# A GNN, linear-attention and mixture-of-experts layer on one core: the mixer's attention rows and queries made one group ahead of its feed-forward, loops written out

## The reference, cut to what matters

```python
xn = _layernorm(x, axis=-1)
x = x + gnn(xn, edge_attr_3, src, dst, ...) + mix(xn[None], ...)[0]
x = x + ffn(_layernorm(x, axis=-1)[None], ...)[0]

# gnn: one message per edge, summed at its destination
m = jnp.concatenate([h[edge_src], w], axis=1)
h_N = jax.ops.segment_sum(jax.nn.relu(m @ W1.T + b1), edge_dst, ...)

# mix: 4 layers over all nodes
for i in range(DEPTH):
    h = _layernorm(x, ln1_g[i], ln1_b[i])
    x = x + _linear_attn(h, Wq[i], Wk[i], Wv[i], Wo[i], bo[i])
    h = _layernorm(x, ln2_g[i], ln2_b[i])
    x = x + (gelu(h @ W1[i] + b1[i], approximate=False) @ W2[i] + b2[i])

# _linear_attn, per head of 32
q = softmax(split(x @ Wq) * scale, axis=-1)
k = softmax(split(x @ Wk) * scale, axis=-2)
context = einsum('bhnd,bhne->bhde', k, v)      # needs every node
out = einsum('bhnd,bhde->bhne', q, context)
```

## Time and profile before

| | |
|---|---|
| median of 3 runs | 2426.01 us (2425.75 to 2429.09) |
| the profiled execution, its own time | 2427.93 us |
| its span (first to last instruction) | 2426.2 us |
| PE, DVE, ACT, POOL busy share | 84%, 64%, 39%, 56% |
| mean granted TensorE clock | 0.921 |
| mixer layers | from about 130 us to 1897 us |

### The profile page before, as it was taken

The page is one execution under the profiler, slowest core; times in us unless marked ns, Lnnn a source line. Parts: engine busy times, 40 slices in busy tenths (PEclk is TensorE's granted clock), DMA queues, the critical chain, the costliest instruction groups (busy, mean ns, idle before and its releaser), DMA issues. The chain is left out here.

```text
span 2426.2 us, 36176 instructions
## 1 busy us (share of the span) xinstructions
PE 2035.1 (84%) x10736; PEld 1661.2 (68%) x10736; DVE 1542.0 (64%) x3503; ACT 951.4 (39%) x1978; POOL 1365.6 (56%) x1118
## 2 busy tenths in 40 slices
PE   2359899998989999898999998899999775699990
PEld 2248677777767777776777777777777564688880
DVE  4658777666876767687777667866766456511116
ACT  1234444443544444443444444444444242133330
POOL 4156666667556666665666666566666400366650
PEclk7769999999999999999999999999999786799995
DMA  8652222224222223332322224222222432599997
GB/s 200 187 136 67 73 67 67 67 67 122 64 71 67 69 72 72 96 83 73 72 67 68 68 71 111 68 66 68 67 71 67 88 96 85 181 302 305 306 289 165
DMA packets 269614, 266.96 MB, mean 110 GB/s; under 512 B 146079, under 2 KB 203510, under 8 KB 269526
## 3 DMA queue, kind: packets, MB, share of 16 engines
q0 software_dynamic: 127488, 134.76, 23.2%
q1 hardware_dynamic: 137926, 131.35, 18.6%
q10 hardware_dynamic: 4112, 0.03, 0.1%
HBM read 229.85 MB, written 35.06 MB: 109 GB/s over the span
## 5 line engine op out<-in xcount | busy, mean ns | idle before, releaser
L780 POOL DMA_INDIRECT G<-P_d,src_T x896 | 1159.2, 1294 | 708.4 <-DVE z L419 428.7
L387 ACT ACTIVATE zr<-z 125x512 fp32r<-125x512 f32 x448 | 275.0, 631 | 551.3 <-DVE z L419 507.9
L419 DVE TENSOR_TENSOR z<-bank,G 125x512 f32<-125x512 f32 x448 | 293.4, 686 | 226.9 <-PE bank L379 96.4
L1190 PE MATMUL bank<-TT,W_s 128*128 128x250 f32 (+1 forms) x1280 | 369.3, 439 | 1.0 <-ACT TT L838 0.9
L1057 PE MATMUL bank<-W_s,hid 128*125 128x256 f32 x1600 | 359.6, 379 | 0.0
L1057 PEld LDWEIGHTS bank<-W_s,hid 128*125 128x125 f32 x1600 | 292.8, 187 | 42.8
L1190 PEld LDWEIGHTS bank<-TT,W_s 128*128 128x128 f32 x1280 | 242.7, 196 | 104.3 <-issue 12.1
L393 DVE SCALAR_TENSOR_TENSOR zl<-z,zr 125x512 fp32r<-125x512 f32 x448 | 288.4, 684 | 8.1 <-ACT zr L387 8.1
L371 PE MATMUL bank<-zr,onehot 125*125 125x256 f32 x896 | 271.3, 334 | 12.8 <-DVE zl L393 12.8
L372 PE MATMUL bank<-zl,onehot 125*125 125x256 f32 x896 | 230.3, 288 | 0.0
L922 ACT ACTIVATE hid<-bank,b1c 128x375 f32<-128x375 f32 x320 | 163.0, 521 | 100.1 <-PE bank L1190 90.5
(11 more groups left out here) (310 smaller groups left out, 3103.4 us busy)
## 6 DMA issues: line engine op xcount, KB each, us to landing
W_s<-in_L_ffn_w SPq DMA_DIRECT2D x64, 512.0 KB
hid<-in_L_ffn_w SPq DMA_DIRECT2D x64, 512.0 KB
G<-P_d,src_T POOLq DMA_INDIRECT x896
W_s<-in_L_mix_W SPq DMA_DIRECT2D x8, 1024.0 KB
aT<-attr_d SPq DMA_DIRECT2D x224, 31.2 KB
attr_d<-hn SPq DMA_DIRECT2D x12, 246.1 KB, 3.7
X<-in_x SPq DMA_DIRECT2D x5, 560.0 KB
P_d<-es SPq DMA_DIRECT2D x25, 112.0 KB
```

What stands on the lines that cost most here:

```text
L387: nc.scalar.activation(zr[:, s, k, :], z[:, k, :], ACT.Relu).then_inc(r_done, 1)
L419: nc.vector.tensor_tensor(z[:, k, :], edge_bank[k][0:ET, :], G[:, ST * s + 2 * k:ST * s + 2 * k + 2, :].rearrange("p j d -> p (j d)"), ALU ...
L780: pool.indirect_dma_start(G[:, j, :], None, P_d[:, :], bass.IndirectOffsetOnAxis(ap=src_T[:, at:at + 1], axis=0)).then_inc(g_in[j], 16)
L1190: ins = pe.matmul(to[:, 0:(b - a) * T], W1_s[:, k, part], TT[:, k, TT_PIECES[pc]], start=k == 0, stop=k == KD - 1)
```

## The change

`second` is dissolved. In the feed-forward section PE's order for group g becomes: blocks f of g with s0 after f=0, s1 after f=2, s2 after f=3, s3 after f=5, s4 after f=7 (`FF_STEP`); first-norm transposes of g+2; query transposes and attention rows of g+1; queries of g+2; output rows piece 0, s5, piece 1, s6, second-norm transposes of g+1 (in the last group: first-norm transposes of the next layer), piece 2, s7. ACT and DVE follow. On DVE the residual and statistics of piece 2, their aggregate and its copy now stand ahead of s7. The middle gets group 0's attention rows and second norm, queries of groups 0 and 1, and 4 steps; the two steps that opened a layer stay in the first layer alone. Each layer's first norm uses statistics that are finished in parts (`deviations`, `inverse_std`). PE's and SP's loops over layers and groups are written out; ACT reads gains and biases where they lie (`lnp`, `b1_s`) in place of copies. Two of the four steps after the layers move into the first layer. No matmul, gather or element of work is added; one ACT copy pair and a full-width `std` a layer go, small `std`s and reciprocals come.

```diff
+        FF_STEP = {0: 0, 2: 1, 3: 2, 5: 3, 7: 4}
...
# PE
-            with pe.Fori(0, L) as l:
+            for l in range(L):
...
+                queries(0)
+                step(eM)
+                pe.wait_ge(cn_done, l + 2)
...
+                normalised_T(l * SETS + set_q1(1) + 0, ring_q1(l, 1))
+                pe.wait_ge(ring_act, uM + 2)
...
+                step(eM + 1)
+                queries_T(0)
+                pe.wait_ge(row_dve, row_ao(l, 0) + 1)
+                attention(0)
+                queries(1)
+                step(eM + 2)
+                normalised_T(l * SETS + set_h2(0), ring_h2(l, 0))
+                step(eM + 3)
...
-                        if f % 2 == 0:
-                            step(f // 2 + 1)
-                    if not last:
-                        normalised(h0 + GT, u0 + GT + LNU + 2 * NF, GT + LNU + 2 * NF)
-                        queries(u0 + GT + LNU + 2 * NF, r0 + NRP, NRP)
-                    step(5)
...
+                        if f in FF_STEP:
+                            step(e0 + FF_STEP[f])
+                    if g + 2 < NG:
+                        normalised_T(l * SETS + set_q1(g + 2), ring_q1(l, g + 2))
+                    if g + 1 < NG:
+                        queries_T(g + 1)
+                        attention(g + 1)
+                    if g + 2 < NG:
+                        queries(g + 2)
...
+                    out_rows(0)
+                    step(e0 + 5)
+                    out_rows(1)
+                    step(e0 + 6)
+                    if g + 1 < NG:
+                        normalised_T(l * SETS + set_h2(g + 1), ring_h2(l, g + 1))
+                    elif l + 1 < L:
+                        normalised_T((l + 1) * SETS, ring_h1(l + 1, 0))
+                    out_rows(2)
+                    step(e0 + 7)
...
# ACT
+                        if f in FF_STEP:
+                            step(e0 + FF_STEP[f])
+                    if g + 2 < NG:
+                        first_norm(ring_q1(l, g + 2), ring_q1(l, g + 2) - RING_A)
+                    if g + 1 < NG:
+                        queries_T(g + 1)
+                        second_std(g + 1)
...
+                    if g + 2 < NG:
+                        q_softmax(g + 2)
+                    step(e0 + 5)
+                    step(e0 + 6)
+                    if g + 1 < NG:
+                        second_norm(g + 1)
...
+                    step(e0 + 7)
# DVE
+                    step(e0)
+                    if g + 2 < NG:
+                        dve.wait_ge(ring_full, ring_h2(l, g) + LNU)
+                        normalised(g + 2)
+                    for i in range(1, 5):
+                        step(e0 + i)
+                    if g + 1 < NG:
+                        attention(g + 1)
+                    if g + 2 < NG:
+                        queries(g + 2)
...
+                    residual(g, r2, 0)
+                    step(e0 + 5)
+                    residual(g, r2, 1)
+                    row_stats(g, r2, 0, st5, a_stat)
+                    step(e0 + 6)
+                    if g + 2 < NG:
+                        q_softmax(g + 2)
+                    residual(g, r2, 2)
+                    row_stats(g, r2, 1, st5, a_stat)
+                    row_stats(g, r2, 2, st5, a_stat)
+                    aggregate(a_stat, a_aggr, l * NT + g * GT + NT, st5, mv5)
+                    keep_stats(g, l * NT + g * GT + NT, a_aggr, a_mv)
+                    step(e0 + 7)
```

More of the change, by code:

```diff
@@ L866, in _, with step @@
                 both(e)
+            def step(ge):
+                act_edges(ge, ge % PG)
             for l in range(L):
[L869 to L875, removed]
@@ new lines, in second_std, with queries_T @@
+                def second_std(g):
+                    act.wait_ge(b_aggr, l * NT + g * GT + GT)
+                    std(std5b[:, :], mv5b[:, :, 1], b_std)
+                def queries_T(g):
+                    u = ring_qT(l, g)
+                    for j in range(GT):
+                        copy_tile(u + j, u + j - RING_A, QT[:, :, j * T:(j + 1) * T], T)
+                if l == 0:
+                    deviations(0, NG, NG)
+                    first_norm(ring_h1(0, 0), 0)
+                    for i in range(ST_A):
+                        step(EG_FIRST * PG + i)
@@ L895, in _ @@
+                    step(step_k(l, g))
                     for j in range(GT):
[L896 to L902 removed]
@@ L903, in _ @@
[L903 to L917 removed]
+                        u = u0 + LNU + 4 + j
@@ L924, in second @@
-                        if f % 2 == 0:
-                            step(f // 2 + 1)
-                    if not last:
-                        normalised(u0 + GT + LNU + 2 * NF, GT + LNU + 2 * NF)
-                    step(5)
-                    if not last:
-                        q_softmax(r0 + NRP, l * NG + g + 1)
-                    step(6)
-                    step(7)
-                for g in range(NG - 1):
-                    second(g)
-                second(NG - 1, last=True)
+                            u = u0 + 2 * f + pc
@@ new lines, in ring, with row_of, rows_at @@
+            def ring(u):
+                pe.wait_ge(ring_act, u - 1)
+                return RING[(u - RING_A) % 3]
+            def row_of(u):
+                pe.wait_ge(row_dve, u)
+                return ROW[(u - ROW_A) % 2]
+            def rows_at(u, i, products):
+                a, b = RP[i]
+                to = row_of(u + i)
+                for j in range(a, b):
+                    pairs = products(j)
+                    for n, (w, m) in enumerate(pairs):
+                        ins = pe.matmul(to[0:T, (j - a) * D:(j - a) * D + D], w, m, start=n == 0, stop=n == len(pairs) - 1)
+                ins.then_inc(row_full, 1)
@@ L1437, in _ @@
                 dve.memset(ctxS[:, :, :], 0.0).then_inc(l_init, 1)
                 dve.memset(mO[:, :], LOW).then_inc(l_init, 1)
[L1439 to L1442 removed]
+                if l == 0:
+                    normalised(0)
+                    for i in range(ST_A):
+                        step(EG_FIRST * PG + i)
                 dve.wait_ge(l_init, l * 2 + 2)
[L1445 to L1447 removed]
+                for g in range(NG):
+                    u0, r0, q0, eg = ring_k(l, g), row_k(l, g), l * (2 * NG) + g * 2, step_k(l, g)
@@ L1575, in _ @@
-                for g in range(NG - 1):
-                    second(g)
-                second(NG - 1, last=True)
+                    r = rM + NRP + h
+                    dve.wait_ge(row_full, r + 1)
+                    dve.tensor_scalar(M_s[:, h, :], ROW[(r - ROW_A) % 2][:, 0:D], rk[:, h:h + 1], None, ALU.mult).then_inc(row_dve, 1)
+                step(eM + 1)
+                attention(0)
+                queries(1)
+                second_norm(0, ring_q1(l, 1) + LNU)
+                step(eM + 2)
```

461 lines of the change are left out of this document (234 added, 227 removed).

## The result

| | before | after |
|---|---|---|
| median | 2427.55 us (2425.75 to 2430.58, 4 runs) | 2554.02 us (2547.77 to 2555.51, 4 runs) |
| ratio | | 1.0506, 95% interval 1.0492 to 1.052 |
| span of the profiled execution | 2426.2 us | 2550.8 us |
| PE, DVE, ACT, POOL busy share | 84%, 64%, 39%, 56% | 81%, 60%, 37%, 54% |

The change costs 126.5 us. I had said 2504 (2432 to 2550): the sign and the cause are right, the size is 50 us short.

The account below looks back on a forecast made before the run. PE, 84% busy, was taken as the bound, with POOL's gathers a near second limit. Middle and feed-forward +110.6, layer changes -29.7, tail -10.8, clock +8 gave 2506 on the profiled 2427.9, so a median of 2504 us (2432 to 2550).

Parts of the forecast that it names:

- the mechanism: Feed-forward groups: POOL's gathers, 6.48 us a step, run unbroken from s7's `z`; PE waits for features behind s4's late data.
- T: Zero point of the forecast's times in a feed-forward group: the end of PE's last output piece.
- Rival (b): Whole kernel: PE keeps its pace, every group drops 3.7 us, 132 us gained in all, 2294 us; chance 0.11.
- the right comparison: Feed-forward group: POOL's run from s7's `z` to s4's data, 29.7 us, against PE's own work there, 22.8.
- step: 38.2: Middle section, from the K section's end to group 0's start point: summed to 38.2 us, ending with a step.
- tail: Steps behind the last layer: two left instead of four, paced by gathers, 20.2 us instead of 31.0, so -10.8.
- loops: PE's loops written out: 0 us, since the old trace showed no idle time between passes.
- So a group takes 70.0: Feed-forward groups 0 to 2, with queries: 70.0 us instead of 64.7; 3.7 of waits go, 9.7 of new ones come.
- +8 (between 0 and 26): PE's low granted clock after new waits: 8 us taken, at most 20 x 1.3 = 26.
- the seam and the K section: Layer change: last rows to first keys 3.6 us instead of 13.5, three times, -29.7, with 3.0 of new waiting.
- +78: Whole kernel: the sum of all terms, +110.6 - 29.7 - 10.8 + 8, on the profiled execution's 2427.9 us.
- rival (d): Whole kernel much slower: clock stays low after longer waits, +26, or SP's `aT` is late, +15; up to 2545; chance 0.07.

Follow-up runs that it names:

- the seam experiment: Steps spread and relus moved, plus on DVE group 1's norm behind the next layer's first two key maxima and V copies, against the kernel without that move: 2395.0 us.

## Why the prediction was wrong in size

**Right: the mechanism.** POOL's run is the path. The prediction's points, with T = 829.92 + 0.11 = 830.03: the run starts at 4.06 (said 3.3) and has no break; s4's last gather is at 27.9 (27.3); its data is read 4.69 later (4.7); the features start at 33.9, where 33.4 was said; the zl wait is 1.18 (1.4), the ROW bank 0.91 (1.0). `z` waits 7.3 us for gathers in the group (over 5). Halving the gathers and spreading the steps each remove the whole gap. Rival (b), PE keeping the pace, was refused on the right comparison. But its price of 132 us is not found where its condition is met: with half the gathers the changed kernel is no faster than the kernel before with half, since waits of 0.62, 1.18, 1.46 and 0.91 us a group stay. Only the spread kernels beat the kernel before, by 1.1 to 1.6%, not by 5%.

**Right by luck: the middle, "step: 38.2".** It takes 38.4 us to the start of its fourth step, PE's timeline in the second layer:

```profile
738.38 0.71 PE L1198 MATMUL bank<-ident,qe 125*128 125x125 f32 x4 [1.97 <-ACT QT L884]
738.92 1.84 PE L1172 MATMUL bank<-M_s,QT 128*125 128x256 f32 x4
...
757.48 1.06 PE L425 MATMUL bank<-Wst,aT 128*125 128x512 bf16 x2
```

The prediction's 38.2 has that step in it, and its group 0 begins with the same step as its s7. So about 1.4 us are counted twice in each layer, and like against like 36.7 stands against 38.4. The miss is of the kind of the others: the attention row takes 1.84 us here and 1.03 at full clock, and the step at 733.05 takes 2.56 where 1.38 was reckoned.

**Right: tail, loops.** Behind the last layer 21.1 us pass (2032.31 to 2053.43) where 20.2 was said and 31.1 stood in the earlier trace rows. Written-out loops gain nothing. The 5.2 us wait for the first norm between layers is gone.

**Mis-sized: the feed-forward groups, "So a group takes 70.0".** They took 71.7 and 71.6 (group 0: 72.5), group 3 64.9 (62.5), group 4 57.3 (54.3): 11.2 us a layer. In the groups with queries the miss has two parts, both in the rows shown. First, `z` of s7 starts at 3.07, not 2.35: the sum left out what DVE issues between the copy and `z`, the register load of the changed order; the row has 0.64 of idle time <-issue there. Secondly, after a wait of 3.22 us the granted clock is low: from 864.6 to 869.0 the windows give it as 0.61, and query transposes with the first attention row take 3.77 us (865.23 to 869.00) where they took 2.36 before (from the first of the earlier trace rows to the row here, where the second attention row begins, PE's timeline of the kernel before; `M_s` is an attention row):

```profile
774.58 1.03 PE L1057 MATMUL bank<-M_s,QT 128*125 128x256 f32 x4
```

PE's timeline of the changed kernel shows the same in group 3, where four matmuls of an attention row take 1.61 us instead of 1.03, and in group 4, where 1.9 us of wait were foreseen and 16 matmuls of output rows take 5.31 us instead of 3.62:

```profile
1007.79 0.71 PE L1198 MATMUL bank<-ident,qe 125*128 125x125 f32 x4 [3.27 <-ACT QT L884]
1008.34 1.61 PE L1172 MATMUL bank<-M_s,QT 128*125 128x256 f32 x4
...
1086.40 0.43 PE L1182 MATMUL bank<-ident,hn 125*128 125x125 f32 x2 [3.07 <-ACT TT L879]
1086.66 5.31 PE L1172 MATMUL bank<-W_s,hid 128*125 128x256 f32 x16
...
1091.92 3.62 PE L1172 MATMUL bank<-W_s,hid 128*125 128x256 f32 x16
```

**Mis-sized: the clock, "+8 (between 0 and 26)".** I had taken it that several waits are on ACT's or POOL's pace, "where a slow PE costs nothing". This is the step that failed most. The long wait *ends* at the features, and what follows it (query transposes, attention rows, queries) is PE's own path. It costs 1.4 us in the rows above, and in each of the 12 groups with queries the same stretch takes 3.55 to 4.03 us, where it took 2.36. An estimate for a layer from rows of the second: three groups with queries at 1.4, group 3 at 1.6, group 4 at 1.7, the K section at 1.5, the middle at 2.9, about 12. That is some 44 us in all (group 4 and the K section have it in three layers), above the bound of 26. The pages bear this out: PE is busy 18.5 us longer for the same matmuls (2053.6 against 2035.1), on top of the 1.3 us a group that the kernel before lost. The digit 9 of the earlier trace rows, which I read as full clock, can't show losses of this size: the mean granted clock of the mixer's layers is 0.96 in both kernels.

**Mis-sized: the seam and the K section.** From the last rows to the end of the K section 94.8 us pass (624.31 to 719.1), where 99.6 - 9.9 = 89.7 was said. PE's timeline at the start of the K section:

```profile
624.31 0.59 PE L425 MATMUL bank<-Wst,aT 128*125 128x512 bf16 x2
...
635.45 1.11 PE L1221 MATMUL bank<-TT,Wk_s 128*128 128x250 f32 x4 [3.65 <-ACT eT L950]
636.40 3.41 PE L1172 MATMUL bank<-Wv_s,TT 128*125 128x256 f32 x8
...
652.00 2.85 PE L1172 MATMUL bank<-Wv_s,TT 128*125 128x256 f32 x12 [0.97 <-DVE ctxS L1641]
...
656.73 1.11 PE L1221 MATMUL bank<-TT,Wk_s 128*128 128x250 f32 x4 [1.03 <-ACT eT L950]
657.67 1.89 PE L1172 MATMUL bank<-Wv_s,TT 128*125 128x256 f32 x8
```

The wait was foreseen in part (3.0 of the 3.65). The low clock behind it was not (eight matmuls of `V` rows in 3.41 us instead of 1.89), nor the second key group's two waits of about 1 us, which the kernel before doesn't have. Those are some 4 of the 5.1 us. The transfer of `aT` was said to be over at T + 12.5; the seam experiment shows it at T + 17.5 (1030.10 against 1012.54 + 0.11). In the changed kernel PE asked at 641.32, T + 17.0, and had no wait in its row: it was hidden only because PE was late too.

**The account.** Short by layer: 8.1, 16.6, 15.2 and 14.5 us, 54.4 in all (layer by layer from the last rows, before and after). Less the +8 that stood for the clock, and with 0.8 by which the tail gave less, that is 47.2 of the 48.5 between +78 and the +126.5 of the medians. The step counted twice made the sum some 5 us larger, so without it the miss would have been about 54. The range's upper end of 2550 stood on rival (d), which had the largest missing piece, a low clock after long waits, at a chance of 0.07. That was not a rival: it follows from the forecast's own waits. Its other piece, a late `aT`, didn't come.

## What to carry to other kernels

Where a slow producer with a shallow buffer feeds steps that are strewn into other work, the spacing of the steps matters as much as their number. With 6.5 us of gathers a step and room for two steps, groups 1 and 2 take 64.1 and 64.0 us when the eight steps are spread, and 71.7 and 71.6 when s7 to s4, six of them, stand within 25 us of PE's own work, with DVE's order the same in both. When a program order is rewritten, write down for each engine what stands directly behind the instruction that may be late: here the same late `z` cost some 40 us where POOL's gathers were on the path, and some 30 us where they weren't, by the traces through ACT's relu with a table load and the GELUs behind it. And if a forecast puts a wait of some 3 us on TensorE's path, the slow matmuls behind it belong to the same term.

The steps spread, with relus moved behind what PE wants (2391.51 us), beat both kernels, by 1.6% and 6.4%. In the second layer its stretches take 196.6, 62.6, 64.1, 55.3 and 48.4 us: against the table above groups 3 and 4 gained 9 us each, since their attention rows or queries are made elsewhere, and 12 of it went to the stretch of K section, middle and group 0.

## What the hardware showed beside this

- A wait of 3.22 us on TensorE was followed by a granted clock of 0.61 over 4.4 us (0.50, the level of 1.2 GHz, from 866 to 868 us; 1.00, the level of 2.4 GHz, from 869), and 1.4 us were lost. In the middle, behind waits of 2.13 and 1.97 us, it was 0.50 from 733.0 to 735.6 us and 0.58 from 738.4 to 742.5; behind one of 1.35 us at 894.30, 16 matmuls took their usual 3.62 us.
- A relu and a load of the GELU table stand between a late `z` and the first GELU on ACT: 1.23 + 1.28 us.
- Writing out loops without taking anything from the path made the kernel before 0.2% slower (ratio 1.001 to 1.003).
